# The second layer reads a block's rows of x from x itself, in two pieces, in place of a padded copy in DRAM

## What is computed

```python
x = x + gnn(layernorm(x), W1, b1, W2, b2, edges)   # gcn_conv, relu, gcn_conv
x = x + ffn(layernorm(x)[None], phi, scale, w1, b1, w2, b2)[0]

def gcn_conv(x, W, b, src, dst, n):      # with a self-loop for each node
    h = x @ W
    deg = segment_sum(ones, dst);  norm = deg[src]**-0.5 * deg[dst]**-0.5
    return segment_sum(h[src] * norm[:, None], dst) + b

def ffn(x, ...):                          # 32 experts with 32 slots each
    logits = l2norm(x) @ (scale * l2norm(phi))
    d_w = softmax over the 32 slots of an expert;  c_w = softmax over all 1024 slots
    slots = d_w^T @ xn;  eo = gelu(slots @ w1 + b1) @ w2 + b2
    return c_w @ eo
```

## Time and profile before

| | |
|---|---|
| median of 3 runs | 3398.86 us (3396.49 to 3400.23) |
| span of the profiled execution | 3527.4 us |
| prepare / first layer / second layer / mixture | about 0-215 / 215-1540 / 1540-2965 / 2965-3527 us |
| PE busy | 3143.9 us, 89% of the span |
| POOL, DVE, ACT busy | 52%, 55%, 34% |
| moved by DMA | 1018.61 MB, 289 GB/s on the mean |

### The profile page before, as it was taken

One profiled execution on the slowest core, in us unless ns is written; L12 is line 12 of the kernel. 1 busy time (PEld: TensorE's weight loads), 2 busy tenths in 40 slices (PEclk: granted clock), 3 DMA queues, 4 the chain that ended last, 5 costly groups with the idle time before them and its releaser, 6 DMA issues. The chain is left out here.

```text
span 3527.4 us, 56846 instructions
## 1 busy us (share of the span) xinstructions
PE 3143.9 (89%) x19474; PEld 2019.7 (57%) x19474; DVE 1942.6 (55%) x2983; ACT 1205.6 (34%) x1447; POOL 1842.0 (52%) x1754
## 2 busy tenths in 40 slices
PE   7237999999999999967999999999999998588998
PEld 7125666666666666634665656665656664244665
DVE  8773444444443444425777877777777775101332
ACT  6951222222222222213444444444444442011000
POOL 0146666666666666536676666776666661100000
PEclk9999999999999999979999999999999999799999
DMA  9488888888888888749998988988889987999996
GB/s 374 180 316 317 293 280 287 303 287 271 298 284 299 293 295 297 263 159 312 313 307 291 311 298 297 312 302 294 288 286 308 308 284 287 340 324 271 277 268 177
DMA packets 344441, 1018.61 MB, mean 289 GB/s; under 512 B 145314, under 2 KB 148668, under 8 KB 335984
## 3 DMA queue, kind: packets, MB, share of 16 engines
q0 software_dynamic: 135776, 660.85, 56.5%
q1 hardware_dynamic: 196916, 322.85, 27.3%
q10 hardware_dynamic: 11484, 31.39, 2.8%
HBM read 854.14 MB, written 135.08 MB: 280 GB/s over the span
## 5 line engine op out<-in xcount | busy, mean ns | idle before, releaser
L1299 POOL DMA_INDIRECT xs<-table,idx x833 | 914.2, 1097 | 501.3 <-PE m_part L1476 214.0
L821 POOL DMA_INDIRECT xs<-table,idx x833 | 878.8, 1055 | 442.9 <-issue 202.9
L1073 PE MATMUL a_part<-xs 128*128 128x512 f16 (+1 forms) x3332 | 592.1, 332 | 76.1 <-DMA xs<-table,idx 52.5
L1476 PE MATMUL m_part<-xs 128*128 128x512 f16 (+1 forms) x3332 | 591.9, 332 | 55.7 <-DMA xs<-table,idx 19.2
L1053 PE MATMUL a_ps_o<-Ws,xs 128*128 128x512 f16 x3528 | 593.1, 326 | 8.9 <-issue 5.5
L1073 PEld LDWEIGHTS a_part<-xs 128*128 128x128 f16 x3332 | 416.3, 142 | 213.2 <-issue 96.9
L1476 PEld LDWEIGHTS m_part<-xs 128*128 128x128 f16 x3332 | 419.3, 142 | 198.4 <-issue 77.3
L1053 PEld LDWEIGHTS a_ps_o<-Ws,xs 128*128 128x128 f16 x3528 | 344.9, 98 | 236.8 <-issue 12.6
L1505 PE MATMUL m_ps_l<-xs,m_xT 128*128 128x512 f16 x1764 | 391.6, 380 | 8.0 <-issue 7.9
L1492 PE MATMUL m_ps_s<-dw_mem,xn_mem 128*128 128x512 f16 x1296 | 312.2, 380 | 3.5 <-DVE xs L1365 3.0
L1505 PEld LDWEIGHTS m_ps_l<-xs,m_xT 128*128 128x128 f16 x1764 | 172.2, 98 | 219.2 <-issue 16.8
(11 more groups left out here) (377 smaller groups left out, 3770.9 us busy)
## 6 DMA issues: line engine op xcount, KB each, us to landing
xs<-in_L_ffn_w_dram SPq DMA_DIRECT2D x64, 1152.0 KB, 11.3
xs<-table SPq DMA_DIRECT2D x98, 384.0 KB
xs<-table,idx POOLq DMA_INDIRECT x1666
cw_dram<-xs SPq DMA_DIRECT2D x49, 512.0 KB
x_pad<-xs SPq DMA_DIRECT2D x7, 2688.0 KB, 23.9
table<-arena SPq DMA_DIRECT2D x49, 384.0 KB, 4.5
table<-xs SPq DMA_DIRECT2D x49, 384.0 KB
xs<-x_pad SPq DMA_DIRECT2D x49, 384.0 KB
```

The source lines that it names most:

```text
L821: pool.indirect_dma_start(out=ring[:, t, :], out_offset=None, in_=table, in_offset=bass.IndirectOffsetOnAxis(ap=idx[:, k:k + 1], axis=0)). ...
L1073: mm = nc.tensor.matmul(part[:, bass.ds(to + a, z - a)], pick[:, i % 2, :, t], ring[:, n % RING, half * D + a:half * D + z], start=False, ...
L1299: pool.indirect_dma_start(out=ring[:, t, :], out_offset=None, in_=table, in_offset=bass.IndirectOffsetOnAxis(ap=idx[:, n:n + 1], axis=0)). ...
L1476: mm = nc.tensor.matmul(part[:, bass.ds(off + at, e - f)], pick[:, i % 2, :, t], ring[:, n % RING, half * D + f:half * D + e], start=False ...
```

## The change

The tensor `x_pad`, its seven stores, the semaphore `x_out` and all waits for it go. In the second layer SP loads a block's rows from x itself. Since x has no rows past 6250, the load is cut in two: rows 0 to 105 of the block, and the remaining 22. For the last block the second piece would lie outside x, so its first row is worked out in registers (`rest`), which for that block alone points to the last 22 rows of x; these land on rows that the kernel masks later. Both pieces count on one semaphore, so DVE waits for 32 in place of 16 per use of the slot.

```diff
-    x_pad = nc.dram_tensor("x_pad", (NBR * P, D), F32).ap()
@@ prepare, SP
                 sp.dma_start(acc[0:TAIL, NBR - 1, :], x[(NBR - 1) * P:N, :]).then_inc(x_in[NBR // XCH - 1], 16)
-                for c in range(0, NBR, 7):
-                    sp.wait_ge(x_in[c // XCH], 32 if c + XCH == NBR else 16)
-                    sp.dma_start(x_pad[c * P:(c + 7) * P, :].rearrange("(b p) d -> p b d", p=P), acc[:, c:c + 7, :]).then_inc(x_out, 16)
                 sp.wait_ge(tab_ready, 1)
...
-                sp.wait_ge(x_out, 16 * 7)
@@ prepare, ACT and DVE, each
-                act.wait_ge(x_out, 16 * 7)
-                v.wait_ge(x_out, 16 * 7)
@@ second_layer, SP
                         wait(sp, x2_out[i % 2], 16 * (i // 2))
-                        sp.dma_start(xb[:, i % 2, :], x_pad[bass.ds(b * P, P), :]).then_inc(x_in[i % 2], 16)
+                        rest = sp.snap(b * P + TAIL - ((b + (64 - NBR + 1)) >> 6) * (P - TAIL)).with_bounds(min_val=TAIL, max_val=N - (P - TAIL))
+                        sp.dma_start(xb[0:TAIL, i % 2, :], x[bass.ds(b * P, TAIL), :]).then_inc(x_in[i % 2], 16)
+                        sp.dma_start(xb[TAIL:P, i % 2, :], x[bass.ds(rest, P - TAIL), :]).then_inc(x_in[i % 2], 16)
@@ second_layer, DVE
-                        v.wait_ge(x_in[j % 2], 16 * (j // 2 + 1))
+                        v.wait_ge(x_in[j % 2], 32 * (j // 2 + 1))
                         v.tensor_tensor(xb[:, j % 2, :], tmp[:, :], xb[:, j % 2, :], ALU.add).then_inc(x2_r, 1)
```

More of the change, by code:

```diff
@@ L132, in gnn_ffn @@
         sems.extend(w_in)
-        prepare(nc, x, src, dst, src_pad, dst_pad, tab_dram, x_pad, xs[:, :].rearrange("p (b d) -> p b d", b=NBR), dloc, idx, tab, dinv, dinv_as,
+        prepare(nc, x, src, dst, src_pad, dst_pad, tab_dram, xs[:, :].rearrange("p (b d) -> p b d", b=NBR), dloc, idx, tab, dinv, dinv_as,
                 lnf, lnb, valid, ident16, iota_x, table1, W1, W2, w_in)
@@ L157, in gnn_ffn @@
             second_layer(nc, table2, idx, dloc, tab, dinv_g, brow2, valid, phi_h, phi_l, scl, slots, ident16, iota_x,
-                         x_pad, x2_dram, cw_dram, rows_mem, sums_mem, misc_mem, w1, w2, w1_first, w1_second, w2_place, w1_in, w2_in,
+                         x, x2_dram, cw_dram, rows_mem, sums_mem, misc_mem, w1, w2, w1_first, w1_second, w2_place, w1_in, w2_in,
                          xn_mem, dw_mem)
@@ L161, in gnn_ffn, with prepare @@
                     iota_x, idx, xn_mem, dw_mem, brow2)
-def prepare(nc, x, src, dst, src_pad, dst_pad, tab_dram, x_pad, acc, dloc, idx, tab, dinv, dinv_as,
+def prepare(nc, x, src, dst, src_pad, dst_pad, tab_dram, acc, dloc, idx, tab, dinv, dinv_as,
             lnf, lnb, valid, ident16, iota_x, table1, W1, W2, w_in):
@@ L293, in prepare @@
         tab_in = sem("tab_in")
-        x_out = sem("x_out")
         totals = sem("totals")
@@ L1150, in spread, with second_layer @@
     return rows.rearrange("p (d c) -> p c d", c=n)
-def second_layer(nc, table, idx, dloc, tab, dinv_g, brow, valid, phi_h, phi_l, scl, slots, ident16, iota_x, x_pad, x2_dram, cw_dram,
+def second_layer(nc, table, idx, dloc, tab, dinv_g, brow, valid, phi_h, phi_l, scl, slots, ident16, iota_x, x, x2_dram, cw_dram,
                  rows_mem, sums_mem, misc_mem, w1, w2, w1_first, w1_second, w2_place, w1_in, w2_in, xn_mem, dw_mem):
```

## The result

The changed kernel takes 3413.32 us (median of 4 runs, 3409.05 to 3419.09), the kernel before on the same occasion 3397.68 us (3394.76 to 3400.23). The ratio is 1.0049, with a 95% interval of 1.0034 to 1.0065: 16 us slower, where the forecast was 78. Ratios leave out the few executions that lie over 1.5% above the fastest of their kernel; medians in the tables don't.

What follows compares the result with a forecast made beforehand. PE was taken as the bound, DMA engines close behind. The second-layer block, midway between 26.5 and 31.5 us plus 0.5, became 29.5 us, 1.6 over 27.9; over 49 blocks +78 on 3399 gave 3477 us, range 3399 to 3550.

Steps and rivals of the forecast that it cites:

- The stores in prepare are worth nothing: Prepare: removing seven stores to x_pad gains 0 us, since normalisation starts 8 us after the last store.
- A transfer of 106 rows runs on two engines: Second-layer load: the 106-row piece puts 53 packets on each of two DMA engines, adding 5.6 us a block with the rest.
- One more DMA in a block costs nothing: Second layer, SP: the extra issue of 0.33 us hides in SP's wait of some 15 us; 0 us.
- A DMA engine has 3.1 us to spare in a block: Second layer: each engine is busy 24.8 us of the 27.9 us period, leaving 3.1 us.
- the upper bound by busy time: Second layer: busy time plus added packets gives 30.4 us a block, or 31.5 us if stalls scale with bytes.
- The lower bound: Second layer: at 25.2 GB/s an engine, 669 KB take 26.5 us, as long as PE, so nothing is lost.
- The half us: Second layer: 0.5 us a block added to 29.0 us because bursts don't fit together, giving 29.5 us.
- +78 us: Second layer: 1.6 us lost in each of 49 blocks, put on the median of 3399 us.
- What would be late next: Second layer: PE waits for gathers 50 us or more; the weights' store, some 5 us late, and own rows stay hidden.
- The sign of being wrong: Second-layer profile: a period of 27.9 us with PE waiting as before would mean engines had more room than busy share says.
- The runs without a profile are 128 us shorter: Whole kernel: profiled span 3527 us against median 3399 us; no row said which phase was shorter.
- the two engines keep up: Second-layer rival: engines carry 669 KB within 27.9 us, so no change, 3399 us; chance 0.12.

Runs made afterwards that it cites:

- e7: Changed kernel with one uncut 128-row load from x per block (last block's added rows shifted by 22), no stores: 3525.25 us, 0.9990 of the kernel before.
- e8: One uncut 128-row load from x per block (last block's rows shifted), with x_pad and its unread stores kept: 3522.00 us, 0.9991 of the kernel before.
- e12: Changed kernel with the load in 96, 10 and 22 rows, and prepare's last load and the final output store cut too: 3509.6 us, 0.9971 of before.
- e17: Kernel before, x_pad and stores kept, second-layer load cut into two pieces of 64 rows: 3519.4 us, ratio 0.9968.
- e4: Changed kernel with the load in 53, 53 and 22 rows, about 108 packets on one engine: 3861.1 us, 1.0926 of the kernel before.
- e16: Changed kernel with the load in 53, 53 and 22 rows, on another chip: 3856.27 us, 1.0893 of the kernel before.
- e9: Changed kernel with the load in 53, 53 and 22 rows, issued by ACT on its own queue: 3838.3 us, 1.0885 of the kernel before.
- e11: Changed kernel with the load in 79, 27 and 22 rows, 84 packets on the fullest engine: 3654.3 us, 1.0352 of the kernel before.
- e5: Changed kernel rerun unaltered on a second chip: 3516.95 us, 0.9973 of the kernel before.
- e10: Changed kernel, load still in 106 and 22 rows but issued by ACT on its own queue: 3525.0 us, 1.0014 of the kernel before.
- e13: Changed kernel rerun unaltered on a fourth chip: 3580.72 us, 1.0110 of the kernel before.
- e1: Kernel before, rerun unchanged for a second profile: 3535.1 us, ratio 1.0002; profiled span 3538.3 us.
- e15: Changed kernel with one uncut 128-row load from x per block (last block's rows shifted), on a fourth chip: 3533.93 us, 0.9980 of the kernel before.

## Why the forecast was right in its sign and wrong in its size

- *The stores in prepare are worth nothing.* Right, and shown: normalisation starts at 120.06 after and 120.16 before, and the medians of e7 and e8 differ by 0.1%, well inside their intervals.
- *A transfer of 106 rows runs on two engines.* Right. The dose (55, 84, 108 packets) and the 4.4 us that ACT gained by 96 and 10 rows in e12 bear it out. For 22 rows no run stands alone.
- *One more DMA in a block costs nothing.* Put at 0 us as hidden on SP. That holds for two pieces of 64 rows (e17), but on two chips three even pieces cost 0.75 points, 26 to 28 us, more than the packets on the two engines did (0.55 points where they could be told apart). So this term failed there, and its cause is open.
- *A DMA engine has 3.1 us to spare in a block.* This is the step that failed, "the upper bound by busy time", and with it the middle of 26.5 and 31.5 us that was taken. The overloaded runs give 5 to 6 us to spare by the estimate of e4 (5.4 in e4, 5.1 in e16, 5.5 in e9, 6.3 in e11), 7 by the knee at 66 packets, where 5.6 were needed. So the share of 0.89 held time that an engine can give up when it has more to do. The lower bound, by the 403 GB/s of the earlier trace rows, was nearest: it said that the engine keeps up. The half us that was added because bursts don't fit together has no row of its own either: the loop after ran within 0.1 us a block of PE's busy time.
- *+78 us.* Mis-sized by a factor of five on the chip of the result: +16, just below the forecast's own lower end of 3414. Nor was the little that is left a loss in each block, as forecast: PE was idle for 5 of 1200 us in the loop. That the sign came true there is thus at least partly luck. On two chips the kernel after or its cut cost 1.0 and 1.1% (+34 and +38 us by the medians), on one (e5) it cost nothing, and nothing on another with the load issued by ACT (e10). The mechanism itself is full-blown only past the knee: +133 us at 84 packets, +313 to +327 at 108.
- *What would be late next.* I expected the gathers alone; the store of the weights was to have some 15 us in hand. In the profile after ACT waits 18.1 us for it in four waits, up to 7.6 each, and in e4 it is the largest wait of ACT. So "both hidden" and "some 5 us late" were too low at times. In e13 it was hidden all the same.
- *The sign of being wrong.* The prediction named it itself: PE waiting as before, "then the engines had more room than their busy share says". That is what the profile after shows, with a DMA share of 0.90 and 304 GB/s where 285 were expected.
- *The runs without a profile are 128 us shorter.* Wrong as a reading: this was the difference between two chips (or occasions), not the profiler (e1). The room of an engine was thus read off a chip on which the kernel is 4% slower than on that of the result.
- *The other rival, "the two engines keep up"* (0.12), describes the second chip (e5) and the third (e10) best, and the loop of the profile after; of the result it explains all but 0.5%.

What stays open: where the 16 us on the chip of the result lie, and which part belongs to the two engines and which to the further piece, since no later run got a chip of that kind and there is no profile of the kernel before on it. By the profile after most of it isn't in PE's waits after 1600 us. The first blocks of the layer are the likelier place: there are 18.4 us of gather waits beyond the fill, and the fill itself took 18.5 us, 18.4 in e13 and 15.2 with one piece (e15). That is an argument, not a test; in e13 the gather waits beyond the fill are only 1.8 us. Open too is why three even pieces cost 0.75% on two chips and nothing on a third.

## What to carry to other kernels

Give the pieces of a transfer row counts that 16, or a number just below it, divides, and look at what the fullest DMA engine has to do: the mean share of the 16 engines fell to 0.71 in e4 while one of them held up the kernel. A single transfer with a bad row count is cheap inside a busy loop with a deep ring, but costs its full 4 to 6 us where somebody waits for it alone, as at the start of a phase or behind the last result; look for those first. The issue itself can hold an engine up when one DMA engine has much queued: 9 us instead of 0.3 in e9. And before the time around a profile is explained, compare a stretch that both programs share.

## What the runs showed of the hardware that I had not expected

The kernel before takes 3398 us on the occasion of the result and 3521 to 3543 us on five other chips. The difference lies in the layers with gathers (1186 us for the first layer's gathers in the fast profile, 1258 to 1276 in the slower ones), while prepare and the mixture agree (603.2 us behind the start of the last addition of x after the change, 604.6 before it). The cost of one and the same cut ranged from -0.3 to +1.1% over these chips, far outside the intervals of single comparisons.

DMA engines recorded as busy 0.89 of the time took some 20 to 25% more work before the loop slowed down (an estimate: 5 to 7 us more in a period of 27.9, where 3.1 us were recorded as idle).
